# Experts' products in halves of TensorE's rows, and frame merging with the projection in one block

## What is computed

```python
# layer 0
x = token_mix(x)                    # per window of 16 frames: q, k, v over frames, softmax -> 8 frames; 2048 rows of 192
u = layernorm(x) * ln_w + ln_b
z, xBC, dt = split(u @ W_in)        # 384 | 640 | 6 columns
xBC = silu(causal_conv(xBC, conv_w) + conv_b)      # 4 taps, sequences of 32 rows
dt = softplus(dt + dt_bias)
h = x + (rmsnorm((ssm_scan(xBC, dt, A) + D * xs) * silu(z)) * norm_w) @ W_out
# mixture of 8 experts, 2 of 8 for each row: gate-weighted gelu(row @ w_fc[e]) @ w_proj[e]    (192 -> 768 -> 192)
# layer 1: causal linear attention with decay, then a mixture of 3 experts, one for each sequence of 32 rows:
#   score * (gelu(row @ W1[e] + b1[e]) @ W2[e] + b2[e]) + residual
```

## Time and profile before

| | us |
|---|---|
| median of 3 runs | 592.81 |
| lowest and highest | 591.47, 593.81 |
| the profiled execution | 597.21 |
| its span, first to last instruction | 595.1 |

### The profile page before, as it was taken

One profiled execution on the slowest core, in us unless ns is written; L12 is line 12 of the kernel. 1 busy time (PEld: TensorE's weight loads), 2 busy tenths in 40 slices (PEclk: granted clock), 3 DMA queues, 4 the chain that ended last, 5 costly groups with the idle time before them and its releaser, 6 DMA issues. The chain is left out here.

```text
span 595.1 us, 12563 instructions
## 1 busy us (share of the span) xinstructions
PE 531.8 (89%) x4135; PEld 472.0 (79%) x4135; DVE 295.7 (50%) x932; ACT 249.0 (42%) x678; POOL 222.8 (37%) x332
## 2 busy tenths in 40 slices
PE   8999799988999729999999999997977737999995
PEld 7677678876887628999999999995977736999975
DVE  2666458777999883233223322322456544333330
ACT  2677656664554232222322232222345541545422
POOL 1244400004997503222112211203877215566731
PEclk9999669998999859999999999997799976999989
DMA  9990000009742101131311311111344321222210
GB/s 259 251 187 4 1 1 1 0 12 287 237 130 77 42 2 48 41 81 50 85 41 42 90 45 42 41 34 47 107 120 147 88 73 47 61 61 61 67 43 24
DMA packets 42701, 45.74 MB, mean 77 GB/s; under 512 B 7665, under 2 KB 37058, under 8 KB 42642
## 3 DMA queue, kind: packets, MB, share of 16 engines
q1 hardware_dynamic: 35682, 31.30, 19.2%
q0 software_dynamic: 6000, 12.30, 7.7%
q10 hardware_dynamic: 960, 1.38, 0.8%
HBM read 29.39 MB, written 10.32 MB: 67 GB/s over the span
## 5 line engine op out<-in xcount | busy, mean ns | idle before, releaser
L1374 POOL DMA_INDIRECT rows_in<-x,token x57 | 57.1, 1002 | 151.6 <-PE psum L1399 126.9
L1420 PE MATMUL psum<-rows_turned,expert_weights 128*128 128x128 f32 x684 | 86.9, 277 | 1.1 <-issue 0.6
L1438 PE MATMUL psum<-w_proj,hidden_room 128*128 x468 | 86.2, 334 | 0.0
L1420 PEld LDWEIGHTS psum<-rows_turned,expert_weights 128*128 128x128 f32 x684 | 81.7, 193 | 2.1 <-issue 1.4
L1438 PEld LDWEIGHTS psum<-w_proj,hidden_room 128*128 128x128 f32 x468 | 75.0, 190 | 4.6
L1461 ACT ACTIVATE hidden_room<-psum 128x384 f32<-128x384 f32 x78 | 34.0, 488 | 76.6 <-PE psum L1424 76.6
L1495 DVE COPY rows_out<-psum 128x192 f32<-128x192 f32 x39 | 13.9, 358 | 104.0 <-PE psum L1438 104.0
L1424 PE MATMUL psum<-rows_turned,expert_weights 64*128 64x128 f32 x684 | 54.9, 292 | 0.0
L1450 ACT ACTIVATE rows_turned<-psum 128x256 f32<-128x256 f32 x57 | 22.1, 388 | 76.0 <-PE psum L1399 70.2
L1424 PEld LDWEIGHTS psum<-rows_turned,expert_weights 64*128 64x128 f32 x684 | 43.8, 189 | 7.1 <-issue 0.2
L714 PE MATMUL psum<-arena 97*128 (+3 forms) x192 | 48.1, 415 | 0.6 <-PEq L403 0.6
(11 more groups left out here) (269 smaller groups left out, 988.0 us busy)
## 6 DMA issues: line engine op xcount, KB each, us to landing
xbc_tile<-xbc SPq DMA_DIRECT2D x16, 320.0 KB, 3.2
w_proj<-in_w_proj SPq DMA_DIRECT2D x8, 576.0 KB, 5.5
y<-rows_out SPq DMA_DIRECT2D x39, 96.0 KB, 1.6
sz<-in_x SPq DMA_DIRECT2D x16, 192.0 KB, 8.1
w_fc<-in_w_fc SPq DMA_DIRECT2D x1, 2304.0 KB, 19.9
w_fc<-in_w_fc SPq DMA_DIRECT2D x3, 768.0 KB, 25.4
w<-in_w SPq DMA_DIRECT2D x3, 576.0 KB
x<-xf_tile SPq DMA_DIRECT2D x16, 96.0 KB, 1.6
```

The source lines that it names most:

```text
L1374: nc.gpsimd.indirect_dma_start(out=x[:, t.odd, 0:D], out_offset=None, in_=src, in_offset=bass.IndirectOffsetOnAxis(ap=tile_token[:, t.i:t. ...
L1420: nc.tensor.matmul(ps_h[t.odd][ch // HALF][:, ch % HALF, :], w_now[:, t.odd, ch * P:(ch + 1) * P], xt[:, t.odd, 0, :], start=ch % HALF == ...
L1438: last = nc.tensor.matmul(ps_y[t.odd], hid[:, t.odd, ch, :], w_down[:, bass.ds((e * HC + ch) * D, D)], start=ch == 0, stop=ch == HC - 1)
```

## The change

1. **Experts.** All products of a tile use 64 rows of the array, in pairs of upper and lower half. The up weights are laid out anew at load (eight pieces instead of four): the upper 64 partitions hold hidden columns 0 to 383 for all 192 inputs in three blocks of 64, the lower ones hidden columns 384 to 767; so the up product is 18 half products. The rows are repeated wholly (`twice`, 384 columns) and turned by six half transposes. The down product is six pairs; the two halves of a pair go to two banks, and DVE adds the two in two steps. DVE copies the down weights of the tile's expert into a fixed buffer as well (`take_second_weights`), PE reads no register. The banks for turned rows and for the result now hold one tile each, no longer two.
2. **Frame merging and projection** are in one block. Chunks 0 to 5 of the first stretch are issued at the end of PE's steps 17 to 22, ACT's first taps and DVE's other taps of three chunks in steps 18 to 22. The loops are written out. ACT's order in the later stretches has the next stretch's first taps between the silus of the one before; the chunk order has gate 1 after the last convolution chunk.

The diff, cut; lines that are taken away and stand in the kernel above are mostly left out:

```diff
-            merge_frames(nc, dram, m, s, banks)
-            project_in(nc, dram, m, s, banks)
+            with ExitStack() as both:
+                merge_frames(nc, dram, m, s, banks, project_in(nc, m, s, banks, both))
...
-STACK_LOADS = 4
+STACK_LOADS = 8
...
+    to = to.rearrange("p (e h) -> p e h", e=n_exp)[:, :, 0:UP].rearrange("p e (b h) -> p e b h", b=3)
     rows = rows.rearrange("p (e c h) -> p e c h", e=n_exp, c=2)
...
+    over, half = HD - LEFT, HID // 2
     for n in range(2):
...
+        first, columns = n * LEFT, slice(n * half, (n + 1) * half)
+        sp.dma_start(to[first:first + LEFT, :, 0, :], rows[0:LEFT, :, 0, columns]).then_inc(loaded, 16)
+        sp.dma_start(to[first:first + over, :, 1, :], rows[LEFT:HD, :, 0, columns]).then_inc(loaded, 16)
+        sp.dma_start(to[first + over:first + LEFT, :, 1, :], rows[0:LEFT - over, :, 1, columns]).then_inc(loaded, 16)
+        sp.dma_start(to[first:first + LEFT, :, 2, :], rows[LEFT - over:HD, :, 1, columns]).then_inc(loaded, 16)
...
+                def project_in(t):
+                    n = t.i - 9
+                    if n == 0:
+                        pe.wait_ge(ones_set, 1)
+                        pe.wait_ge(w_low, 4)
+                        pe.wait_ge(row_low, 2)
+                        pe.wait_ge(ut_low, 4)
+                        pe.wait_ge(qk_ev, TILES - 1)
+                    elif n == 1:
+                        pe.wait_ge(qk_ev, TILES)
+                    elif n == 2:
+                        pe.wait_ge(h_out, TILES)
+                    elif n == 3:
+                        pe.wait_ge(s_min, TILES)
+                    elif n == 4:
+                        pe.wait_ge(pt_ev, TILES)
+                    elif n == 5:
+                        pe.wait_ge(c_ev, TILES)
+                        pe.wait_ge(b_done, TILES)
+                    if 0 <= n < 6:
+                        projection.chunk(pe, 0, n)
+                pipelined(pe, TILES, [(3, mix_frames), (6, turn_u), (7, steps), (1, score), (0, project), (2, turn_probs), (3, attend), (4, bias_row), (8, project_in)], 8, straight=True)
+                pe.wait_ge(ut_kept, TILES)
+                pe.wait_ge(ut_low, TILES)
+                projection.chunk(pe, 0, 6)
+                pe.wait_ge(dt_out, TILES)
+                projection.chunk(pe, 0, 7)
+                projection.tensor(pe)
...
+                projection.exp_a(act)
...
+                def first_taps(t):
+                    c = {10: 0, 11: 1, 13: 2, 14: 3}.get(t.i)
+                    if c is not None:
+                        projection.first_tap(act, 0, c)
+                pipelined(act, TILES, [(5, norm), (5, add_normed), (6, take_u), (1, exponent), (2, take_probs), (3, take_h), (2, w_in_high), (4, row_high_part), (8, first_taps)], 8, straight=True)
+                act.wait_ge(o_mm, TILES)
+                projection.scalar(act)
...
+                def other_taps(t):
+                    c = {11: 0, 12: 1, 14: 2}.get(t.i)
+                    if c is not None:
+                        projection.taps(dve, 0, c)
                 pipelined(dve, TILES, [(3, take_mix), (3, bias_of_h), (4, sum_rows), (1, bar_and_least), (4, moments), (6, low_part), (7, take_dt), (0, take_qk), (1, invert),
...
+                                       (1, normalise), (3, w_in_low), (4, row_low_part), (8, other_taps)], 8, straight=True)
                 dve.wait_ge(m.loaded, 16)
+                dve.wait_ge(dt_out, TILES)
+                projection.vector(dve)
...
+    chunks = [("conv", 0, 3), ("conv", 1, 4), ("gate", 0, 0), ("conv", 2, 5), ("conv", 3, 6), ("conv", 4, 7), ("gate", 1, 1), ("gate", 2, 2)]
...
+    def chunk(pe, j, n):
+        kind, c, ch = chunks[n]
+        if j and kind == "conv":
+            pe.wait_ge(taps_done, 3 * (5 * (j - 1) + c + 1))
+        elif j:
+            pe.wait_ge(gate_out, 3 * (j - 1) + c + 1)
+        for half, w, u in terms:
+            k = HD + 1 if half == 0 and u == 0 else HD
+            last = nc.tensor.matmul(bank_of[kind][c][:, :], s.w_parts[0:k, w, half, ch * P:(ch + 1) * P], s.ut_parts[0:k, u, half, tokens(j)],
+                                    start=(half, w, u) == terms[0], stop=(half, w, u) == terms[-1])
+        last.then_inc(proj, 1)
+    def tensor(pe):
+        for j in range(1, STRETCHES):
+            for n in range(len(chunks)):
+                chunk(pe, j, n)
+        pe.wait_ge(taps_done, 3 * (5 * (STRETCHES - 1) + 1))
+        stay_busy(nc, banks[0][:, 0:P], m.c["ident"], 28)
+    def first_tap(act, j, c):
+        act.wait_ge(proj, 8 * j + at["conv", c] + 1)
+        need(act, conv_silu, 5 * (j - 1) + c + 1)
+        act.activation(pre[:, c, :], banks[c][:, :], ACT.Identity, bias=p["conv_b"][:, c:c + 1],
+                       scale=p["conv_w"][:, 4 * c + 3:4 * c + 4]).then_inc(tap3, 1)
...
+        act.wait_ge(mag_done, 1)
+        act.activation(ex[:, :], mag[:, :], ACT.Exp, scale=-1.0).then_inc(exp_done, 1)
+        first_tap(act, 0, 4)
+        act.wait_ge(one_done, 1)
+        act.activation(ln1[:, :], one_ex[:, :], ACT.Ln).then_inc(log_done, 1)
+        act.activation(warm[:, :], p["A_log"][:, 0:1], ACT.Silu)
+        gate(0, 0)
+        for j in range(1, STRETCHES):
+            silu(j - 1, 0)
+            first_tap(act, j, 0)
+            gate(j - 1, 1)
+            silu(j - 1, 1)
+            first_tap(act, j, 1)
+            gate(j - 1, 2)
+            silu(j - 1, 2)
+            first_tap(act, j, 2)
+            silu(j - 1, 3)
+            first_tap(act, j, 3)
+            gate(j, 0)
+            silu(j - 1, 4)
+            first_tap(act, j, 4)
...
+        silu(STRETCHES - 1, 4)
...
+    def vector(dve):
+        nc.vector.scalar_tensor_tensor(mag[:, :], m.dt[:, :], -1.0, m.dt[:, :], ALU.mult, ALU.max).then_inc(mag_done, 1)
+        taps(dve, 0, 3)
+        dve.wait_ge(exp_done, 1)
+        nc.vector.tensor_scalar(one_ex[:, :], ex[:, :], 1.0, None, ALU.add).then_inc(one_done, 1)
+        dve.wait_ge(one_done, 1)
+        nc.vector.tensor_scalar(back[:, :], one_ex[:, :], -1.0, None, ALU.add).then_inc(back1, 1)
+        dve.wait_ge(back1, 1)
+        nc.vector.tensor_tensor(mag[:, :], ex[:, :], back[:, :], ALU.subtract).then_inc(back2, 1)
+        taps(dve, 0, 4)
+        dve.wait_ge(back2, 1)
+        dve.wait_ge(log_done, 1)
+        nc.vector.tensor_tensor(one_ex[:, :], ln1[:, :], mag[:, :], ALU.add).then_inc(back3, 1)
+        dve.wait_ge(back3, 1)
+        nc.vector.scalar_tensor_tensor(m.dt[:, :], m.dt[:, :], 0.0, one_ex[:, :], ALU.max, ALU.add).then_inc(sp_done, 1)
+        dve.wait_ge(sp_done, 1)
+        dve.wait_ge(ea_done, 1)
+        nc.vector.scalar_tensor_tensor(m.dt_a[:, :].rearrange("p (i h) -> p i h", h=NH), m.dt[:, :].rearrange("p (i h) -> p i h", h=NH), -1.0,
+                                       e_a[:, :].unsqueeze(1).to_broadcast([P, TILES, NH]), ALU.mult, ALU.mult).then_inc(a_done, 1)
+        for j in range(1, STRETCHES):
+            for c in range(5):
+                taps(dve, j, c)
...
+    BLOCKS = D // LEFT
+    x = sb("rows_in", [P, 2, D])
+    twice = sb("rows_twice", [P, 2, BLOCKS, 2, LEFT])
+    xt = sb("rows_turned", [P, 2, BLOCKS, P])
     hid = room[:, 0:2 * HID].rearrange("p (o c n) -> p o c n", o=2, c=HC)
...
+    w_down_now = sb("expert_second_weights", [P, 2, HC * D])
...
+    act_done, y_out, w_down_set = sem("gelu_ready"), sem("rows_ready"), sem("expert_second_weights_set")
+    x_mm, x_out, up_mm, down_mm = ([sem(f"{n}_first"), sem(f"{n}_last")] for n in ("rows_turned_mm", "rows_turned_out", "up_product", "down_product"))
+    halves = [slice(n * LEFT, (n + 1) * LEFT) for n in range(2)]
+    ps_h = [[ps[:, b, 0:HALF * P].rearrange("p (c t) -> p c t", c=HALF) for b in pair] for pair in ((0, 1), (2, 3))]
+    ps_x = [ps[:, b, 0:D].rearrange("p (c t) -> p c t", c=BLOCKS) for b in (4, 5)]
+    ps_y = [ps[:, b, 0:D] for b in (6, 7)]
...
-            need(pool, x_mm, t.i - 1)
...
         stay_busy(nc, ps[:, 7, 0:P], c["ident"], 7 if merge else 12)
...
         def turn_rows(t):
             pe.wait_ge(x_twice, t.i + 1)
-            need(pe, x_out, t.i - 1)
...
+            for half in range(2):
+                need(pe, x_out[half], t.i)
+            for block in range(BLOCKS):
+                for half, at in enumerate(halves):
+                    done = nc.tensor.transpose(ps_x[half][:, block, :], twice[at, t.odd, block, :, :].rearrange("p a d -> p (a d)"), c["ident"][at, at])
+                    if block == BLOCKS - 1:
+                        done.then_inc(x_mm[half], 1)
         def up(t):
             if t.i == 0:
                 stay_busy(nc, ps[:, 7, 0:P], c["ident"], 3)
             pe.wait_ge(w_set, t.i + 1)
...
+            for half in range(2):
+                pe.wait_ge(x_out[half], t.i + 1)
             need(pe, act_done, HC * (t.i - 1))
+            for block in range(BLOCKS):
+                for ch in range(HALF):
+                    first = (block * HALF + ch) * P
```

(48 more changed lines are left out.)

235 lines of the change are left out of this document (65 added, 170 removed).

## The result

In the measurement that belongs to the prediction, the changed kernel takes 569.8 us in the median against 593.3, a ratio of 0.9593 (95% interval 0.9547 to 0.964): **24 us less**, where 30.9 were forecast. A ratio leaves out runs that lie over 1.5% above the fastest run of their kernel, here one of 587.2 us. The same kernel was measured twice more, on two different chips, and there it took 581.5 us (before 593.3) and 602.2 us (before 597.4). So there are two things to explain: why 24 and not 31 us, and what takes the gain away there.

A forecast was written before the change was run, and what follows sets the result against it. TensorE was taken to bound the expert tiles, a chain through all engines the frames' end. Savings of 11 (frames and projection), 15.9 (stage one) and 4.0 (stage two), 30.9 from the median 592.8, gave 561.9 us, range 555 to 578.

The forecast's parts named there:

- Turns of mode, -0.40 us a tile: Expert tile on TensorE: changes between full and half-row products cost 0.40 us, which all-half products save.
- A term of 0.43: Expert tile: total saving forecast, 0.43 us (0.28 at least), for a tile of 4.14 us, at most 4.30.
- half-row pair of 192 columns: Down product: pair to pair taken as 0.162 us, the full product's step; at most 0.21.
- The transposes: Expert tile: six half transposes in three pairs at 0.059 us, 0.18 us instead of 0.22.
- a half's next load does run beside its product: Half products on TensorE: loads overlap products; by the contrary rule 7.3 us a tile, given no chance.
- Stage two, period 4.30 from GpSimd: Second experts: three transfers a tile, slowed by VectorE's copies, set a 4.3 us period; 4.9 us saved, 4.0 after ends.
- VectorE in the experts: Stage one: 3.7 to 4.0 us of work a tile, hidden under 4.14; another engine becoming the bound had chance 0.17.
- Frames and projection, 11 us: Merged block: first-stretch chunks inside the frames' last steps bring the state space to about 121 us, saving 11 (8 to 13).
- Clock 1.0 from 62 us on: TensorE from the frames' end: full granted clock from 62 us on, named as a sign that the forecast is right.
- half of that is lost: 8: Frames and projection: if the clock rises as late as before, 5.4 us after the dense start, only 8 us are saved.
- Rival C, TensorE's supply: Experts: the sequencer can't feed 66 loads and products a tile, 4.95 us a tile, 605 us in all; chance 0.05.
- The ends of the stages, -0.85 each: Both expert stages: later first up product (0.4 us) and a second evacuation at the last tile (0.42) cost 0.85 a stage.

The follow-up runs named there:

- warm_14: Changed kernel with 14 instead of 28 warming products at the projection's end, second chip: 577.4 us, ratio 0.974 to the kernel before.
- projection_only: Kernel before with only the merged block of frame merging and projection from the change, first chip: 589.6 us, ratio 0.9873.
- full_down: Changed kernel with one full product for each half pair in the down product, first chip: 613.5 us, no ratio.
- after_third: The changed kernel, unaltered, measured on the third chip: 602.2 us, kernel before 597.4 there, no ratio.
- experts_again: Kernel before with only the experts and their weights' loads from the change, second chip: 578.0 us, ratio 0.9748.
- after_again: The changed kernel, unaltered, measured on the second chip: 581.5 us, ratio 0.9805 to the kernel before.
- chunks_after: Changed kernel with the first stretch's chunks and taps behind the frames' last step, second chip: 578.8 us, ratio 0.9768.

## Why the prediction was right, and where its sizes were off

The forecast was 561.9 in a range of 555 to 578; the time is 569.8. The mechanism of the experts holds everywhere in stage one. That the whole lies in the range is in part luck: the first measurement kept the clock through the chunks and had no late products in stage two. Where one or both went the other way the same kernel took 581.5 and 602.2 us, outside the range. Point by point:

- **Turns of mode, -0.40 us a tile: right.** 0.39 by taking them out of the kernel before, 0.34 by putting them back into the changed one. The tile came to 4.197, not 4.14: the up product 2.06 for 2.02 (its first step 0.05 longer), the down product 1.953 for 1.94. A term of 0.43 that measured 0.378, over 39 tiles 2 us. The half-row pair of 192 columns, for which the trace had no row, takes 0.1625 us, the lower bound that I took. The transposes: 0.18, as taken. A pair starts every 0.112 us, each product with a load of its own half, as in the full-row product: a half's next load does run beside its product.
- **Stage two, period 4.30 from GpSimd: wrong, and to the safe side.** The timeline of GpSimd in the changed kernel, two gathers:

```profile
519.28 1.09 POOL L1439 DMA_INDIRECT rows_in<-x,token  x1 [0.31 <-issue]
...
523.22 1.24 POOL L1439 DMA_INDIRECT rows_in<-x,token  x1 [0.30 <-issue]
```

  With 3.94 from gather to gather here, GpSimd keeps up with 4.20. I took the period by adding two slowed transfers to 3.83; one gather in the earlier trace rows was slow already. Stage two saved some 5 us beside before's disturbance (8.7 - 3.9), forecast 4.0.
- **VectorE in the experts: size wrong, verdict right.** Counted 3.7 to 4.0 us a tile, measured 2.67: a copy of 1152 columns takes 0.76 in stage one and not 0.98, and the idle time before the copy, which I counted as VectorE's work (0.47 to 0.84), went away with the tighter order.
- **Frames and projection, 11 us: 8.8 in the first measurement.** The last dt step is at 78.05, as put (78.0). But six chunks do not lie *before* it: the sixth starts at 78.16. So three chunks follow, not two, and the stretches start at 82.46 instead of 80.8. Then 24 chunks take 1.41 us each: products end at 116.5, forecast 114.5. That is the term of the frames that was mis-sized, by 2 us. And the forecast took TensorE's 6.4 us of warming as given; 3.3 of them lie behind all other work, which warm_14 got back.
- **"Clock 1.0 from 62 us on": a condition, treated as an outcome.** The bound for it ("half of that is lost: 8") took only the projection's start into account. With the chunks in the frames' chain, a fall at 64 us costs 9.6 us (123.19 to 132.81, two profiles of one kernel; on the first chip 11.0, from projection_only's 122.54 to full_down's 133.50) and leaves nothing of the 8.8. It fell in five of the seven profiles that have the merged block as the change has it. The state of the clock was named in the prediction as what would show it right or wrong, and should have been a rival with a price: 561.9 + 9.6 = 571.5 by what the runs show.
- **Rival C, TensorE's supply: rejected, and its sign came on two of the three chips.** It was to decide at 0.072 us for a load with its product. Stage one needs 4.197 / 66 = 0.064 and has it everywhere. Stage two on the third chip had in after_third (last less first transposes, 87.9 us over 16 tiles) / 66 = 0.083. Nothing in the trace of before would have told it apart from the earlier trace rows: one product 0.85 us late on "issue", which I put down to a disturbance and left out of the sum, is the same sign, at 38 products a tile.
- **The ends of the stages, -0.85 each**: +0.5 us ahead of the first tile and +1.6 from the last transposes of stage one to the first gather of stage two, about as forecast in all.

Together: 2 us in the frames and projection, 2 in stage one's tile, 1 to 2 at its ends, and the 2.6 us by which the profile of before was short in its state space, which only the spans show. The parts add up where the clock stayed up and stage two was clean: 9.4 us (projection_only) and 15.3 (experts_again) are 24.7, the change gave 24. The three numbers are of three measurements, not all on one chip, so this is a rough check.

## What to carry to other kernels

Keep TensorE's products in one mode through a tile: the two changes between full and half rows cost 0.34 to 0.39 us a tile here, and a half pair costs no more than a full product, though it costs twice the instructions. Look at where the work that is moved will lie in the clock's history: here the work put right behind a thinly filled stretch ran at whichever clock that stretch left, so fill the thin steps first, and price both clocks. When instructions a us go up, measure on more than one chip; a product late on "issue" in the profile before, as in the earlier trace rows, may be the warning.

## What the runs showed of the hardware that I had not expected

- The same kernel, with the same work before the point, has its granted clock fall at 63.8 us in one execution and not in another, and its state space then starts 9.6 us later. The runs beside the profiled one were mostly alike (after_again 579.8 to 584.4 us at a mean clock of 0.915 to 0.926), but not always: after_third has one run of 592.2 us at 0.940 and three of 602.1 to 605.5 at 0.910 to 0.922. What decides it stays open.
- After a fall the half clock lasted 24 to 27 us in the merged block, though TensorE reads busy without idle time there (27.00 of 27 us in full_down), and 17 us in chunks_after, where its dense run of chunks starts at 77.0 instead of 85.6.
- Products and weight loads late by 0.2 to 1.4 us with nothing waited for, in stage two, on two of the three chips and in every kernel profiled there. In stage one, on the second chip and in the changed kernel's first profile only a stage's last down product comes late by as much (1.0 and 1.2 us in that profile); the kernel before had the one near 570 us.
- A GpSimd gather takes 1.28 us in the mean in the changed kernel and 1.00 before (L1439, L1374). The second weights' copy on VectorE may be the reason, which no run tests; it had no price here.
